# Graph layer: accumulator cleared by GpSimd, raw rows normalised ahead of the row bounds

## What is computed

```python
h = jnp.maximum(_layernorm(x, axis=-1), 0.0)
ea = edge_attr @ W_edge.T + b_edge
msg = jax.nn.relu(h[src] + ea)
aggr = jax.ops.segment_sum(msg, dst, num_segments=N_NODES)
z = (1.0 + eps) * h + aggr
z = jax.nn.relu(z @ W1.T + b1)
out = x + z @ W2.T + b2
```

## Time and profile before

| what | us |
|---|---|
| timed runs, median of 3 | 1079.86 (1077.92 to 1081.59) |
| profiled execution, span from first to last instruction | 1239.1 |
| profiled execution, time outside the span | not given |
| busy time of POOL in the span | 785.9 |
| busy time of PE in the span | 628.9 |
| busy time of DVE in the span | 518.5 |

### The profile page before, as it was taken

One profiled execution on the slowest core, in us unless ns is written; L12 is line 12 of the kernel. 1 busy time (PEld: TensorE's weight loads), 2 busy tenths in 40 slices (PEclk: granted clock), 3 DMA queues, 4 the chain that ended last, 5 costly groups with the idle time before them and its releaser, 6 DMA issues.

```text
span 1239.1 us, 9124 instructions
## 1 busy us (share of the span) xinstructions
PE 628.9 (51%) x2786; PEld 515.6 (42%) x2786; DVE 518.5 (42%) x658; ACT 193.0 (16%) x233; POOL 785.9 (63%) x838
## 2 busy tenths in 40 slices
PE   2226544455554454555554555444555545554568
PEld 2215434344433334444444444343444434443456
DVE  6645344444433333354344333333343444333373
ACT  5102111111111111111111111111111111111114
POOL 6756666666666666666666666666666666666540
PEclk9999666665656665565665656655556565565668
DMA  8513222333222223333333332222222333232212
GB/s 217 145 33 94 66 64 67 74 85 74 67 67 67 68 67 75 72 73 75 74 93 95 76 74 66 67 67 67 64 66 68 74 88 72 68 67 61 49 29 78
DMA packets 51183, 93.30 MB, mean 75 GB/s; under 512 B 17722, under 2 KB 20443, under 8 KB 51136
## 3 DMA queue, kind: packets, MB, share of 16 engines
q0 software_dynamic: 26592, 40.85, 16.3%
q1 hardware_dynamic: 24390, 51.63, 15.2%
q10 hardware_dynamic: 154, 0.24, 0.1%
HBM read 87.85 MB, written 4.80 MB: 75 GB/s over the span
## 4 chain that ended last, share of the span: by engine, by line
another core or an unknown queue 56%; DVE 23%; issue 8%; DVEq 8%; PE 3%; DMA 1%; ACT 0%; SPq 0%; ACTq 0%
DVE edge_ps L854 7%; DVE edge_ps L865 5%; DVE msg_parts L879 4%; DVEq L768 3%; DVE acc L759 2%; DVEq L770 2%; DVE acc L849 1%; PE edge_ps L601 1%; DVEq L762 1%; DVE stats L639 1%; PE edge_ps L462 1%; DVEq L795 1%; DVE select L705 1%; DVEq L783 1%
## 5 line engine op out<-in xcount | busy, mean ns | idle before, releaser
L352 POOL DMA_INDIRECT gathered<-h_table,src_all x810 | 764.5, 944 | 396.4 <-issue 234.7
L462 PE MATMUL edge_ps<-w_edge,edge_in 97*128 97x96 f32 x1660 | 403.6, 392 | 521.4 <-issue 517.1
L462 PEld LDWEIGHTS edge_ps<-w_edge,edge_in 97*128 97x128 f32 x1660 | 361.8, 302 | 565.0 <-issue 564.1
L787 DVE TENSOR_REDUCE sums<-agg_ps 128x192 f32<-128x576 f32 x41 | 31.0, 757 | 590.4 <-remote 590.4
L424 ACT ACTIVATE msg_parts<-edge_ps 128x960 bf16<-128x960 f32 (+1 forms) x83 | 79.2, 957 | 970.1 <-DVE edge_ps L865 704.4
L543 PE MATMUL agg_ps<-msg_parts,select 128*128 128x288 bf16 x816 | 167.9, 386 | 6.4 <-issue 6.4
L705 DVE TENSOR_TENSOR select<-const_ps,dst_rel 128x2560 bf16<-128x2560 f32 (+1 forms) x43 | 120.8, 2812 | 34.8 <-issue 28.5
L543 PEld LDWEIGHTS agg_ps<-msg_parts,select 128*128 128x128 bf16 x816 | 109.4, 134 | 60.9 <-issue 8.1
L865 DVE TENSOR_TENSOR edge_ps<-edge_ps,gathered 128x960 f32<-128x960 f32 (+1 forms) x83 | 90.9, 1141 | 47.9 <-remote 42.8
L854 DVE SCALAR_TENSOR_TENSOR edge_ps<-edge_ps,msg_parts 128x960 f32<-128x960 f32 (+1 forms) x83 | 91.1, 1144 | 0.3 <-issue 0.3
L879 DVE TENSOR_TENSOR msg_parts<-edge_ps,msg_parts 128x960 bf16<-128x960 f32 (+1 forms) x83 | 90.8, 1136 | 0.3 <-issue 0.3
(11 more groups left out here) (73 smaller groups left out, 143.1 us busy)
## 6 DMA issues: line engine op xcount, KB each, us to landing
edge_in<-edge_t_dram SPq DMA_DIRECT2D x165, 240.0 KB
gathered<-h_table,src_all POOLq DMA_INDIRECT x810
x_all<-x_dram SPq DMA_DIRECT2D x5, 420.0 KB
h_all<-x_dram SPq DMA_DIRECT2D x10, 210.0 KB
out_dram<-h_all SPq DMA_DIRECT2D x10, 210.0 KB
h_table<-h_all SPq DMA_DIRECT2D x3, 420.0 KB
h_table<-h_all SPq DMA_DIRECT2D x1, 630.0 KB
dst_by_row<-dst_rows_dram SPq DMA_DIRECT2D x1, 480.0 KB, 4.2
```

What stands on the lines that cost most here:

```text
L352: nc.gpsimd.indirect_dma_start(out=gathered[c % SLOTS][:, at:at + D], out_offset=None, in_=table, in_offset=bass.IndirectOffsetOnAxis(ap=s ...
L462: mm = pe.matmul(edge_bank(c, g)[:, (k - k0) * D:(k - k0 + 1) * D], edge_in[c % SLOTS][:, k * EDGE_TILE:(k + 1) * EDGE_TILE], w_edge[:], s ...
```

## The change

- POOL clears `sums` and `acc` between its 13th and 14th raw gather. DVE no longer does so in `prepare_sums`.
- DVE sets both rows of ones at its start. ACT's copy and PE's wait for it are gone.
- DVE normalises all of batch 0's raw rows and adds the first messages before it takes the row bounds. The two reductions over `dst_by_row` now stand after `add_rows(0)` and after `take_high(0)`.
- POOL's first pacing wait, ahead of batch 2, is for the finished edge features of batch 1 (`edge_done` at 2) instead of the begun ones (`edge_begun` at 2).

```diff
--- before.py
+++ after.py
@@ -169,7 +169,6 @@
         iota_made = sem("iota_made")
         iota_copied = sem("iota_copied")
         ones_set = sem("ones_set")
-        ones_copied = sem("ones_copied")
         hidden_ones_set = sem("hidden_ones_set")
         dve_step = sem("dve_step")
         var_ready = sem("var_ready")
@@ -357,6 +356,8 @@
             pool.wait_ge(src_first_in, 16)
             for k in range(FIRST_BURST):
                 gather(x, 0, k)
+            nc.gpsimd.memset(sums[:], 0.0).then_inc(sums_made, 1)
+            nc.gpsimd.memset(acc[:], 0.0).then_inc(acc_summed, 1)
             pool.wait_ge(norm_ready, len(LN_PARTS))
             for k in range(FIRST_BURST, tiles_of[0]):
                 gather(x, 0, k)
@@ -367,7 +368,9 @@
                 in_offset=bass.IndirectOffsetOnAxis(ap=src_all[0:TAIL, TILES:TILES + 1], axis=0),
             ).then_inc(tail_gather_in, 16)
             for c in range(1, BATCHES):
-                if c >= SLOTS:
+                if c == SLOTS:
+                    pool.wait_ge(edge_done, c)
+                elif c > SLOTS:
                     pool.wait_ge(edge_begun, c)
                 for p, (k0, k1) in enumerate(pairs[c]):
                     last_use = used_by(c, p, SLOTS)
@@ -408,8 +411,6 @@
             act.wait_ge(h_by_act, ACT_PARTS)
             for a, b in spread:
                 act.dma_start(table_dram[a:b, part_of(own)], h_all[a:b, part_of(own)]).then_inc(table_stored, 16)
-            act.wait_ge(ones_set, 1)
-            nc.scalar.copy(edge_in[1][D:D + 1, :], edge_in[0][D:D + 1, :]).then_inc(ones_copied, 1)
 
             for k, (t0, t1) in enumerate(RAW_PARTS):
                 cols = slice(COLS + t0, COLS + t1)
@@ -569,8 +570,6 @@
                 elif c >= 1:
                     sum_windows(c - 1)
                 if c + 1 < BATCHES:
-                    if c == 0:
-                        pe.wait_ge(ones_copied, 1)
                     edge_features(c + 1)
             sum_late_windows(LAST)
             all_summed = pe.snap(window)
@@ -615,7 +614,8 @@
             nc.vector.memset(eps_col[:], LN_EPS)
             nc.vector.memset(w2[:, D:WINDOW], 0.0)
             nc.vector.memset(dst_rel[:, TILES + 1:TILES + 1 + MOST], 0.0)
-            nc.vector.memset(edge_in[0][D:D + 1, :], 1.0)
+            for edges in edge_in:
+                nc.vector.memset(edges[D:D + 1, :], 1.0)
             nc.vector.memset(edge_tail_in[D:D + 1, :], 1.0).then_inc(ones_set, 1)
 
             def combine(of, at, count, parts):
@@ -694,12 +694,14 @@
                 return nc.vector.tensor_scalar(rows, rows, 0.0, None, ALU.max)
 
             raw_var(0)
-            dve.wait_ge(dst_rows_in, 16)
-            nc.vector.tensor_reduce(first_last[:, 0:1], dst_by_row[:], AX.X, ALU.min).then_inc(bounds_min_max, 1)
             raw_normalise(0)
             raw_var(1)
-            nc.vector.tensor_reduce(first_last[:, 1:2], dst_by_row[:], AX.X, ALU.max).then_inc(bounds_min_max, 1)
             ordered(raw_normalise(1))
+
+            def row_bound(k):
+                dve.wait_ge(dst_rows_in, 16)
+                nc.vector.tensor_reduce(first_last[:, k:k + 1], dst_by_row[:], AX.X,
+                                        (ALU.min, ALU.max)[k]).then_inc(bounds_min_max, 1)
 
             def make_select(b, at, tiles):
                 nc.vector.tensor_tensor(
@@ -736,8 +738,6 @@
                 dve.wait_ge(offsets_made, 1)
                 make_select(0, 0, tiles_of[0])
                 make_select(1, first_tile[1], tiles_of[1])
-                nc.vector.memset(sums[:], 0.0).then_inc(sums_made, 1)
-                nc.vector.memset(acc[:], 0.0).then_inc(acc_summed, 1)
 
             window = dve.alloc_register("dve_window")
             dve.reg_mov(window, 1)
@@ -884,7 +884,11 @@
                 if c >= 1:
                     bounds = load_bounds(c - 1)
                 add_rows(c)
+                if c == 0:
+                    row_bound(0)
                 take_high(c)
+                if c == 0:
+                    row_bound(1)
                 take_middle(c)
                 if c == TAIL_AT:
                     dve.wait_ge(tail_edge_done, 1)
```

## The result

| kernel | median, us | runs |
|---|---|---|
| before | 1079.23 (1077.92 to 1081.59) | 5 |
| changed | 1085.48 (1083.76 to 1085.98) | 5 |

The ratio is 1.0049 with a 95% interval of 1.0037 to 1.0060: the change costs about 5.3 us (4.0 to 6.5). This is slower by more than 0.3%, where the likeliest case of the forecast had it within. The measured 1085.48 lies inside the stated range of 1074 to 1086, 0.5 us from its end.

The account below looks back on a forecast made before the run. The prediction took POOL's back-to-back table gathers as the bound. It added 2.0 us for the memsets on POOL and 0 for each of the four other terms to 1079.86, giving 1081.9 us, range 1074 to 1086.

Parts of the forecast that it names:

- likeliest case: Whole kernel: 1081.9 us, with a range of its own from 1078.5 to 1083.1; within 0.3% of before, chance 0.52.
- What bounds the kernel: POOL's back-to-back table gathers; the profile's waits, 161.8 us, are nearly absent from timed runs, since 1239.1 less 161.8 is 1077.3.
- The memsets' own time: POOL's queue in the head: clearing `sums` and `acc` takes 5.7 us in all, 5.4 of it for `acc`.
- Rival 2: POOL's memset in the head: clears slowly at 1.46 ns per column, giving 1083 to 1087, say 1085 us; chance 0.07.
- I take **2.0**, nearer the upper end: Cost of POOL's memsets ahead of the table gathers: 2.0 us, chosen between 0 and 3.2.
- The bound of 3.2: Upper end for the memsets on POOL: 3.2 us, if the head has no stalls and the table is stored at 30.4.
- Rival 1: Head: POOL's memset blocks DVE's 15 table rows, adding up to 5.6 us to the table, 1085.5 us; chance 0.15.
- The rows of ones: DVE's start: the second memset of 2.19 us hides in the 2.33 us wait for `x`; cost 0.
- The raw rows ahead of the bounds: DVE's early chain: 14 us earlier in all at the second batch, but worth 0 unless POOL waits for it.
- The later wait ahead of batch 2: POOL ahead of batch 2: `edge_done` reaches 2 near 59, POOL arrives at 62; cost 0, or 3.8 us if late.
- Rival 3: POOL ahead of batch 2: batch 1's mark is late in timed runs too, 3.8 us more, 1085.7 us; chance 0.06.
- rival 4: POOL's waits are real in timed runs and DVE's earlier chain shortens batch 3's: faster, say 1075 us; chance 0.20.

Follow-up runs that it names:

- e1: The kernel before, unchanged, run again for a second profile: 1078.63 us against 1078.57, ratio 1.0002, span 1075.9 us.
- e2: The kernel before with only the two memsets moved to POOL between the 13th and 14th raw gather: 1081.58 us, ratio 1.0029.
- e4: The kernel before with four extra raw gathers into an unused tile between the 13th and 14th, memsets still on DVE: 1081.71 us, ratio 1.0028.
- e5: The kernel before with the two memsets on POOL behind its 20th raw gather: 1082.89 us, ratio 1.0039.
- e6: The kernel before with only the second row of ones moved from ACT to DVE's start: 1079.42 us, ratio 1.0005.
- e10: The kernel before with DVE's part of the table made and stored in two pieces, 8 and 7 columns: 1078.70 us, ratio 1.0002.
- e9: The kernel before with half of the accumulator cleared by POOL between the 13th and 14th raw gather, the rest and the sums by DVE: 1079.54 us, ratio 0.9999.
- e13: The kernel before with both memsets on POOL between the 13th and 14th raw gather and the accumulator cleared twice: 1088.45 us, ratio 1.0093.
- e11: The kernel before with only the raw rows moved ahead of the row bounds on DVE: 1079.82 us, ratio 1.0004.

## Why the prediction was wrong in its likeliest case

The forecast was 2.0 us, to 1081.9, and 5.3 were measured. The range of 1074 to 1086 held the result by luck: the forecast's own case ended at 1083.1, and the rest of the range was there for rivals 1 to 3. Two of these didn't happen, and the price of the first was wrong.

- **What bounds the kernel** was read rightly: POOL issues table gathers back to back, and the long waits belonged to the one profile. The sum behind it was wrong, though. Each of the 40 waits takes the place of the usual 0.3 us behind a gather, so they lengthen the kernel by 149.6 us and not by 161.8, as the stretches from the first to the last table gather show (1159.65 us in the first profile, 1010.00 in e1). 1239.1 less 149.6 is 1089.5. The other 13.6 us of the difference to e1's span are a first table gather 3.8 us later and an end of 43.6 us instead of 33.9. That the estimate of 1077.3 came so near to the median and to the span of 1075.9 was luck, two errors of 12 and 14 us against each other; only e1 shows the reading.
- **The memsets' own time**: 5.7 us forecast; 5.62 measured from 18.91 to the end at 24.53. Rival 2, a slow clear, falls: the memset takes 5.43 us for 6378 columns, as DVE's does (5.37). The sentence of the Trainium skill ("GPSIMD Engine Reference", section "Key points"), that VectorE is about twice as fast at elementwise work, doesn't hold for a memset here.
- **The step that failed** is "I take **2.0**, nearer the upper end". The bound of 3.2 was the answer: 3.20 us at the first table gather in the change, 3.2 in e2. The argument behind the bound (no stalls in the head, so that 1.0 us of cover becomes none) was right: it put the statistics at 19.0, and e1 has 18.95. Hedging it with a disturbed profile was the mistake. By the second profile the cost is the memsets' 5.6 to 5.7 us less the idle time of 0.4 + 2.6, plus some tenths of a longer gather and start: 2.7 to 3.2.
- **What had no term**: the table gathers themselves. The stretch from the first to the last grew by 1.15 us, and three of them took 1.24, 1.24 and 1.69 us instead of 0.94 to 0.97. The first two (35.24, 43.03) began 0.2 to 0.3 us after DVE began the 0.66 us maximum over raw rows (34.97, 42.79). In run e1 the same two maxima began 0.3 and 0.1 us behind the start of a gather (38.59 against 38.31, 45.99 against 45.91), and those gathers took 1.06 and 0.94. So it is how the two fall against each other that counts, not a new piece of work. The third and longest, at 54.57, began 0.1 us after these rows of DVE:

```profile
54.44 1.22 DVE L730 TENSOR_TENSOR dst_rel<-dst_all,bounds_f 128x800 f32<-128x800 int32 x4
```

The same rows stand behind the gather of about 1.56 us in e2, e4, e5, e6 and e10, which begins 0.3 us after they do. In e1, e9 and e13 the gather begins 0.9 us after they do and takes 0.94 to 0.96. In all profiles up to 62 us, no gather that began under the `dst_rel` rows ended sooner than 0.6 us after them, and none that began under a maximum (over raw rows or over the table) sooner than 0.8 us after it. The 0.4 us outside the span had no term either.
- **Rival 1**, the blocked rows, had its mechanism confirmed and its price refuted. One row took 4716 ns (5635 in e2), and the 15 rows ended at 28.2 instead of 22.7. The rule of the Trainium skill ("SBUF — State Buffer", section "Who interferes with whom"), that a GpSimd instruction and a VectorE operation in a 2-port mode hold the shared pair for a whole instruction, agrees with that row; in which mode the row ran, no trace shows. But the forecast of 1085.5 added the 5.6 us to the time of the stored table, and the table came only 3.2 to 3.3 us later (SP's next issue at 33.21 against 30.02 in e1 and 29.89 in e5), since the store of the last part took 4.1 us behind the late row and 6.4 in e1. That is within 0.1 us of what the queue costs by itself, so the rival's mechanism reaches POOL but adds nothing. That the median came out near this rival's number is no evidence for it: e4 and e5 have the cost without the block.
- **The rows of ones**: cost 0 forecast; up to 1 us at the statistics, no difference in the time that can be told (e6).
- **The raw rows ahead of the bounds**: 0, right (e11). The chain came forward by 6.3 us, not by 14. DVE's first statistics of raw rows began 5.4 us later (29.03 against 23.59 in e1), mostly because of the held row, and it then waited another 1.1 us for the later raw gathers; the prediction took DVE's delay by the memset at nothing. Its slack was 7.6 us already.
- **The later wait ahead of batch 2**: 0, right, but with little to spare. SP, which waits for the same `edge_done`, issued at 61.16, and POOL's first gather of the batch stood at 61.55 behind its usual 0.3. No run has this edit alone.
- **Rival 3** (a late mark, 3.8 us) and **rival 4** (real waits, faster) fall with run e1.

As a sum: 3.2 (memsets) + 1.1 (the stretch of table gathers) gives the 4.3 us by which the last table gather is late, and 0.4 outside the span makes it 4.7, inside the intervals of both comparisons (4.0 to 6.5 and 3.3 to 6.5).

## What to carry to other kernels

An engine whose queue is the bound pays in full for every instruction that is moved onto it, beyond the idle time that it has ahead of its next binding wait: here 3.0 us, so that half an accumulator was free, a whole one cost 3 us and two cost 9 to 10. Look also for a second thing that becomes late by the same move: here the table and the queue end together, so taking the block away (e5) won nothing back. Measure that idle time in a profile whose span agrees with the timed runs. When a profile's span far exceeds the median and repeated waits account for most of the excess, don't use the cover that it shows; take the bound that follows without those waits. When such waits are added up, only what goes beyond the usual gap counts.

## What the runs showed of the hardware that was not expected

- The same program gave profiles with spans of 1239.1 and 1075.9 us, with equal timed medians. In the longer one SP and DVE, which both wait for the end of batch 1's edge features, went on together at 92.26 and 92.27, 26.8 us after the last of these matmuls, and POOL's next wait ended at 98.95. In e1 SP went on at 61.71, and the matmuls ended at 61.68. Why the mark was late, is open.
- A GpSimd memset of 5.43 us makes a single VectorE row of 96 columns, which takes about 0.32 us otherwise, last 4.7 us (5.6 in e2), and one of 2.77 us makes it last 2.7.
- The stored table followed DVE's last row by 6.4 us when that row ended at 23.7 and ACT's store left at the same time, and by 4.1 when it ended at 29.1 and its store left alone. The time of a store isn't a constant in this head.
- A gather of 0.94 us that begins under one of VectorE's maxima ends no sooner than 0.8 us after it (28.20 + 0.91 and 28.44 + 1.49 in the change), and one that begins under the `dst_rel` rows no sooner than 0.6 us after them. One that begins 0.1 us ahead of such a maximum (45.91 in e1) takes its usual 0.94.
- The same kernel with the accumulator cleared by POOL has 0.3 to 0.4 us more outside its span (2.1 to 2.2 us against 1.8 to 1.9).
- The stretch behind the last table gather takes 33.6 to 37.4 us, at a mean granted clock of 1.00 to 0.84 in it.
